# One step later for the softmax chain and the half ends, two for the terms, and single distances over a longer preparation

## What is computed

```
q    = grouped_conv1x1(bn(x), qw)                           # 8 groups of 16 channels
off  = tanh(pw @ gelu(depthwise_conv6x6_stride4(q))) * 4    # 8x8 sampling points a group
kv   = bilinear_sample(bn(x), grid + off);  k, v = conv1x1(kv)
pos  = grid_q - grid_kv                                     # 1024 queries x 64 keys x 2
bias = w3 @ relu(w2 @ relu(w1 @ (sign(pos) * log1p(|pos|)) + b1) + b2) + b3
out  = softmax(q k / 4 + bias) @ v;   x = x + out_w @ out;   x = x + mlp(bn(x))
```

## Time and profile before

| | before |
|---|---|
| median of 3 runs | 892.25 us (891.63 to 893.71) |
| the profiled execution: its own time, its span | 894.96 us, 893.2 us |
| PE busy | 820.4 us (92%) |
| DVE busy | 727.8 us (81%) |
| ACT busy | 662.1 us (74%) |
| GpSimd busy | 62.5 us (7%) |
| granted TensorE clock, mean | 0.983 |

### The profile page before, as it was taken

How to read it: one execution, slowest core, us unless ns; L and a number is a source line. 1 busy time by engine, 2 the same in 40 slices (tenths; PEclk the granted TensorE clock), 3 DMA queues, 4 the chain that set the end, 5 groups by cost and what they waited for, 6 DMA issues and landing times.

```text
span 893.2 us, 27554 instructions
## 1 busy us (share of the span) xinstructions
PE 820.4 (92%) x12486; PEld 235.6 (26%) x12486; DVE 727.8 (81%) x532; ACT 662.1 (74%) x742; POOL 62.5 (7%) x39
## 2 busy tenths in 40 slices
PE   4699998889999999988999999988999999999997
PEld 2222222222222222222222222222222222222224
DVE  5899898898868689799885879979888668989843
ACT  2468778968777688896776877797777668888863
POOL 1000101000010100101010010100101001010110
PEclk8699999999999999999999999999999999999999
DMA  4502020020200102002020200102002020200000
GB/s 167 118 3 49 2 48 3 12 66 2 63 15 17 34 3 49 12 19 49 2 62 15 48 1 14 37 12 57 11 5 60 14 48 3 73 3 3 3 15 24
DMA packets 18264, 27.67 MB, mean 31 GB/s; under 512 B 10980, under 2 KB 11620, under 8 KB 18148
## 3 DMA queue, kind: packets, MB, share of 16 engines
q1 hardware_dynamic: 18148, 25.91, 11.7%
HBM read 23.05 MB, written 2.74 MB: 29 GB/s over the span
## 4 chain that ended last, share of the span: by engine, by line
PE 68%; ACT 14%; DVE 10%; issue 7%; DMA 1%; SPq 0%; ACTq 0%; POOLq 0%
PE pair L887 24%; PE scores L905 22%; ACT h L481 7%; PE pair L861 6%; DVE h L629 5%; PE pair L1040 3%; PE scores L916 3%; PE pair L995 2%; DVE big L742 2%; PE pair L1031 2%; PE pair L1013 2%; PE scores L1001 1%; ACT big L548 1%; ACT big L577 1%; ACT L577 1%
## 5 line engine op out<-in xcount | busy, mean ns | idle before, releaser
L629 DVE TENSOR_TENSOR h<-hxy 128x2048 f32<-128x2048 f32 x256 | 582.6, 2303 | 71.8 <-PE pair L887 67.8
L481 ACT ACTIVATE h<-pair 128x1024 f32<-128x1024 f32 x512 | 518.7, 1025 | 154.3 <-PE pair L861 113.5
L887 PE MATMUL pair<-h,wts 32*32 32x512 f32 x8192 | 300.0, 604 | 20.7 <-DVE h L629 7.7
L905 PE MATMUL scores<-h,wts 128*32 128x512 f32 x2048 | 275.6, 608 | 0.1
L463 POOL CAST neg_max_wide<-neg_max 128x512 fp32r<-128x512 f32 x32 | 59.3, 1853 | 808.0 <-DVE neg_max L765 808.0
L861 PE MATMUL pair<-fy,u_rows 32*128 32x512 bf16 x1024 | 102.6, 387 | 0.0
L887 PEld LDWEIGHTS pair<-h,wts 32*32 32x32 f32 x8192 | 66.0, 103 | 82.1 <-ACT h L481 36.2
L861 PEld LDWEIGHTS pair<-fy,u_rows 32*128 32x128 bf16 x1024 | 26.4, 91 | 217.2 <-issue 217.2
L905 PEld LDWEIGHTS scores<-h,wts 128*32 128x32 f32 x2048 | 42.0, 108 | 156.2 <-issue 147.5
L995 PE MATMUL pair<-const,probs 128*128 128x128 f32 x128 | 20.1, 280 | 21.6 <-ACT h L481 20.8
L491 ACT ACTIVATE probs<-scores,wts 128x512 f32<-128x512 f32 x32 | 22.0, 689 | 23.7 <-PE scores L905 23.5
(11 more groups left out here) (106 smaller groups left out, 359.9 us busy)
## 6 DMA issues: line engine op xcount, KB each, us to landing
hxy<-features_dram SPq DMA_DIRECT2D x64, 256.0 KB, 4.8
wts<-weights_dram SPq DMA_DIRECT2D x2, 960.0 KB, 8.3
att_den<-reciprocals_dram SPq DMA_DIRECT2D x7, 256.0 KB
x<-x_dram SPq DMA_DIRECT2D x2, 512.0 KB, 5.7
fy<-fy_dram SPq DMA_DIRECT2D x16, 64.0 KB
fy_dram<-fy_part SPq DMA_DIRECT2D x24, 32.0 KB, 3.9
out_dram<-x SPq DMA_DIRECT2D x3, 256.0 KB, 5.4
features_dram<-pos_sign SPq DMA_DIRECT2D x4, 128.0 KB, 2.5
```

The costliest lines, as they stand in the source:

```text
L481: emptied("z", 2 * g + j, act.activation(h2[j][g % H2_BUFS][:].rearrange("p r n -> p (r n)"), pair_of("z", 2 * g + j)[:], ACT.Relu))
L629: dve.tensor_tensor(h1[g % H1_BUFS][:].rearrange("p c (y x) -> p c y x", x=W), hx[unit % 2][:, :, t].unsqueeze(2).broadcast_to([128, CT, H ...
L887: ins = pe.matmul(z_of(g, r)[32 * c:32 * (c + 1)], w(l, "w2")[key_rows(r), key_rows(r)], h1[g % H1_BUFS][key_rows(r), c], start=r >= 2, st ...
L905: ins = pe.matmul(scores[phase % 2][32 * r:32 * (r + 1)], w(l, "w3")[:, 32 * t:32 * (t + 1)], h2[rows[0] // 2][step % H2_BUFS][:, r % 2], ...
```

## The change

The softmax stages behind the copy, and all stages of `AFTER_SLOTS`, stand one step later; `fy_weights` and `hidden_terms` stand one and two steps later. `distances` now emits one activation a call and is called eight times instead of four, and the preparation from `image_t` on is given other steps, the last one 60 instead of 51. No instruction is added or left out. Cut, of the tables a line or two:

```diff
 BEFORE_SLOTS = {
...
-    ("act", "features", 0): 37, ("act", "spread_out", 0): 37, ("dve", "features_sign", 0): 40,
...
+    ("dve", "positions", 0): 39, ("pe", "spread", 0): 39, ("act", "features", 0): 38, ("act", "spread_out", 0): 39,
...
-SOFTMAX_SLOTS = {("pe", "scores_t"): 2, ("dve", "score_max"): 4, ("pool", "widen_max"): 3,
-                 ("pe", "max_off"): 4, ("act", "exp"): 4}
-TERMS_SLOT = 12
+SOFTMAX_SLOTS = {("pe", "scores_t"): 3, ("dve", "score_max"): 5, ("pool", "widen_max"): 4,
+                 ("pe", "max_off"): 5, ("act", "exp"): 5}
+TERMS_SLOT = 14
...
-    put("dve", 21, "fy_weights", 1)
+    put("dve", 22, "fy_weights", 1)
...
             def distances(n):
 
-                wait_emptied(act, "spread", n // 4)
-                for k in (2 * (n % 4), 2 * (n % 4) + 1):
-                    act.activation(hat_y[:, k], key_y, ACT.Abs, bias=cst("neg_y")[:, k:k + 1]).then_inc(distances_ready, 1)
+                k = n % CHUNKS
+                wait_emptied(act, "spread", n // CHUNKS)
+                act.activation(hat_y[:, k], key_y, ACT.Abs, bias=cst("neg_y")[:, k:k + 1]).then_inc(distances_ready, 1)
```

More of the change, by code:

```diff
@@ L83 @@
[L83 to L86, removed]
+    ("dve", "norm1", 0): 28, ("pe", "q", 0): 28, ("act", "q_out", 0): 28, ("dve", "conv_products", 0): 32,
+    ("dve", "conv_products", 1): 33, ("pe", "image_t", 0): 31, ("act", "image_t_out", 0): 31, ("dve", "conv_sum", 0): 34,
@@ new lines @@
+    ("dve", "conv_sum", 1): 35, ("act", "conv_gelu", 0): 35, ("pe", "offset", 0): 36, ("act", "offset_tanh", 0): 36,
+    ("dve", "positions", 0): 39, ("pe", "spread", 0): 39, ("act", "features", 0): 38, ("act", "spread_out", 0): 39,
+    ("dve", "features_sign", 0): 41, ("act", "distances", 0): 40, ("act", "distances", 1): 42,
+    ("act", "distances", 2): 43, ("act", "distances", 3): 44, ("act", "distances", 4): 46, ("act", "distances", 5): 47,
+    ("act", "distances", 6): 48, ("act", "distances", 7): 50, ("dve", "hats", 0): 47, ("dve", "hats", 1): 52,
@@ L87 @@
+    ("dve", "hat_products", 0): 48, ("dve", "hat_products", 1): 54, ("pe", "sample", 0): 55, ("dve", "sample_out", 0): 57,
+    ("pe", "keys_values", 0): 60, ("act", "keys_values_out", 0): 60,
 }
 AFTER_SLOTS = {
-    ("pe", "attend", 0): 5, ("act", "attend_out", 0): 5, ("dve", "reciprocal", 0): 9, ("dve", "divide", 0): 12,
-    ("pe", "project", 0): 12, ("dve", "residual1", 0): 14, ("pe", "mlp_up", 0): 14, ("act", "mlp_gelu", 0): 14,
-    ("pe", "mlp_up", 1): 15, ("act", "mlp_gelu", 1): 15, ("pe", "mlp_down", 0): 17, ("dve", "residual2", 0): 19,
-}
@@ L96 @@
-SOFTMAX_SLOTS = {("pe", "scores_t"): 2, ("dve", "score_max"): 4, ("pool", "widen_max"): 3,
-                 ("pe", "max_off"): 4, ("act", "exp"): 4}
-TERMS_SLOT = 12
+    ("pe", "attend", 0): 6, ("act", "attend_out", 0): 6, ("dve", "reciprocal", 0): 10, ("dve", "divide", 0): 13,
+    ("pe", "project", 0): 13, ("dve", "residual1", 0): 15, ("pe", "mlp_up", 0): 15, ("act", "mlp_gelu", 0): 15,
+    ("pe", "mlp_up", 1): 16, ("act", "mlp_gelu", 1): 16, ("pe", "mlp_down", 0): 18, ("dve", "residual2", 0): 20,
+}
@@ L100 @@
+SOFTMAX_SLOTS = {("pe", "scores_t"): 3, ("dve", "score_max"): 5, ("pool", "widen_max"): 4,
+                 ("pe", "max_off"): 5, ("act", "exp"): 5}
+TERMS_SLOT = 14
 PROLOGUE = {
     "pe": ["q", "image_t", "offset", "spread", "u_rows"],
-    "act": ["q_out", "image_t_out", "conv_gelu", "offset_tanh", "features", "spread_out"] + ["distances"] * 4,
+    "act": ["q_out", "image_t_out", "conv_gelu", "offset_tanh", "features", "spread_out"] + ["distances"] * 8,
     "dve": ["norm1", "w1y_rows", "conv_products", "conv_products", "conv_sum", "conv_sum", "positions", "features_sign",
```

## The result

The changed kernel takes 907.12 us (median of 4 runs, 906.37 to 908.18) against 892.14 (891.63 to 893.71) for the kernel before: a ratio of 1.0155 with a 95% interval of 1.0136 to 1.0174. It is **15 us slower**, where 13 us faster was forecast, and the result lies outside the forecast's range (868 to 889). The profiled execution took 908.18 us, its span is 906.4 us, and the mean granted clock fell from 0.983 to 0.968.

What follows compares the result with a forecast made beforehand. PE, busy 92% of the span, was taken to bound the kernel, so only its waits could move. Gains 5.7 + 6.0 + 1.1 + 0.9 - 0.7 = 13.0 off 892.25 gave 879.2 us, range 868 to 889.

Steps and rivals of the forecast that it cites:

- the last sentence on the quiet phases: Quiet phases: maxima, widening, `max_off` and exponential keep their distances from the transposes; no cost priced.
- The sentence on the terms: Terms two steps later: worth nothing; with cover gone they would cost up to 1.9 us a unit.
- quiet transposes: Quiet phases, softmax one step later: 19 transposes each gain 0.3 us of wait, 5.7 us, bounds 3.8 and 6.8.
- half ends: Half ends one step later: 0.35 us per half shrinks by 0.18, six halves, gain 1.1, bounds 0 and 2.1.
- The long waits at the transposes: Preparation, steps 35 and 43: waits of 2.05 and 1.65 us go; transposes' waits total 1.0 in place of 4.5.
- `spread`: Preparation, step 39: `spread` waits 2.3 us instead of 1.1 for a relu behind `features`; ends 0.1 and 3.5.
- Step 52: Preparation: PE's second layer waits 2.2 us for the maxima, against 1.8 for DVE before; ends 0 and 3.5.
- The clock: Each preparation: one fall to half clock, costing 1.7 us; ends 0 and 3.4.
- rival 1: Preparation gives its gain back: clock falls behind both long waits, `spread` waits its upper end; about 888 us, chance 0.18.
- the price of 884.3: Preparations: time in us if every wait as long as 2.05 us drew a clock fall, 3 x 1.7 more.
- Tail: End of the kernel: last maxima behind `divide` come 0.7 us later, a loss of 0.7, ends 0 and 1.5.
- Rival 3: Preparation, step 52: second `hats` wait for a late distance, holding first layer and maxima; 894 us or more, chance 0.08.

Runs made afterwards that it cites:

- version with the wait: The changed kernel plus a DVE wait, ahead of the second four products, for GpSimd's widening of that phase; 888.61 us, ratio 0.9944.
- version with both repairs: The changed kernel with DVE's second products waiting for GpSimd's widening, and `features` in step 39 instead of 38; 879.4 us, ratio 0.984.
- the filler runs: The fastest version plus one or three useless DVE instructions ahead of the maxima in seven phases of segment 3; 874.75 and 875.88 us.
- the fastest version: The changed kernel with `features` in 39, second `hats` in 53, all products (54, 56) behind a wait for the widening, `sample` 57; 874.15 us.

## Why the prediction was wrong

**The step that failed** is the last sentence on the quiet phases: "The maxima, the widening, `max_off` and the exponential keep their distances from the transposes." They do, in the tables, and so were priced at nothing. But the widening's *duration* is not its own: it depends on what DVE does behind the maxima. The cover that was not named was this: in every other phase of the old order the terms stood right behind the maxima, and in the rest the second first layer gave way to the cast or DVE paused ahead of it, so that no cast was longer than 2.62 us. The change moved the terms away and filled the time ahead of the maxima of 53, so that DVE reached them late, with four products and three first layers in a row behind them and none that gave way: casts of 9.42 us, 13.1 us of waits of PE in step 53 and a long fall of the clock in each preparation, 18.5 us in all by the run in which the products wait. The sentence on the terms ("nothing") is the same mistake.

Result and forecast lie 28 us apart (907.1 and 879.2). The 9.4 us that the collision in step 53 leaves open can be estimated from what follows: two falls of the clock more than priced in the version with the wait (3.4), step 37 (2.6), the quiet transposes (1.3) and the half ends (1.1), 8.4 together.

- *Quiet transposes* (forecast 5.7): right in mechanism. In the changed kernel they start 1.28 us after the second layer, without a wait:

```profile
816.65 1.17 PE L886 MATMUL pair<-h,wts 32*32 32x512 f32 x32
...
819.13 1.17 PE L886 MATMUL pair<-h,wts 32*32 32x512 f32 x32
820.41 0.63 PE L994 MATMUL pair<-const,probs 128*128 128x128 f32 x4
```

 instead of 1.55. But the step of the copy now lasts 2.48 instead of 2.42, which was not in the sum: steps 2 and 3 together fall from 5.86 to 5.63, 0.23 a phase, 4.4 for 19.
- *The long waits at the transposes*: gone, as said; 0.7 left in segment 1.
- *`spread`*: its wait was forecast at 2.3 and is 2.17, by the mechanism that was given (ACT of the changed kernel, the four instructions of `features` ahead of the relus):

```profile
372.78 0.41 ACT L527 ACTIVATE pos_abs<-pos 128x256 f32<-128x256 f32 x1
...
375.27 1.92 ACT L480 ACTIVATE h<-pair 128x1024 f32<-128x1024 f32 x2
...
376.42 2.02 PE L963 MATMUL pair<-const,coord 128*128 128x128 f32 x16 [2.17 <-ACT h L480]
```

- *Step 52*: its wait was forecast at 2.2 and is 1.97. *Step 36*: forecast 0.6, measured 0.42.
- *The clock*: one fall a preparation was priced (1.7). There were three, two and three, some of them 6.8 us long. The wait for the cast accounts for the long ones; but the product-wait version, without it, still has five falls in three preparations, behind `spread` and behind the maxima. So rival 1 was nearer here: without the collision in step 53 the change gives 888.61, near its 888, though only one half of its mechanism is there, as `spread` waits 2.17 us and not its upper end of 3.5. Nor does every wait as long draw a fall, as the price of 884.3 needs: `spread` waited 2.17 us in all three segments, and no fall followed in segment 1 (in the version with the wait, in segment 0).
- *Half ends* (forecast 1.1): not seen. Steps 0 to 27 of segments 1 to 3 shrink by 0.63 each, less than the four quiet transposes in them would give (0.92). The waits for the gelu are gone (2.0 us over six half ends), but `mlp_down` (L1039) now waits for a relu at each of the six, 1.8 us in all, and did not before. *`fy_weights`*: segment 0 shrinks by 1.89 there, 0.97 more than that 0.92, which fits the 0.9.
- *Tail* (forecast a loss of 0.7): 0.5. `divide` still sits behind its DMA, and the last maxima have lost their room of 1.75 us:

```profile
882.22 0.69 DVE L778 TENSOR_TENSOR work<-att_sum,att_den 128x512 f32<-128x512 f32 x1 [5.13 <-DMA att_den<-reciprocals_dram]
882.83 0.68 DVE L764 TENSOR_REDUCE neg_max<-pair 128x8 f32<-128x512 f32 x1
```

- *Rival 3*, the slower one, had the right price (PE waits over 3 us a preparation, and the clock falls a second time) one step too early, in 52, and the wrong mechanism: nothing waited for the hats.

The version with both repairs lands at 879.4, the forecast's figure, by chance: it removes a cost that the sum had counted (`spread`) along with the one that it had not.

## To carry to other kernels

Before moving a short GpSimd instruction that PE needs, look at what DVE does right behind its start: its length can be set by DVE's next break, and the break may be a stage that you are moving away. Where DVE is late, a break may not come in time; make a stage of DVE that is not urgent wait for GpSimd's result, which here cost 0.58 us of DVE's time a preparation and won 18.5 us in all. An engine that is not busy is no proof that its instruction is safe: GpSimd was idle for 93% of the span.

## What the hardware showed

**GpSimd gets no fair turn beside DVE.** The cast alone takes 0.62 us. Beside DVE it took 1.13, 1.54, 2.61, 4.81, 5.14, 7.01, 9.42 and up to 9.97 us: where DVE had more to do, it ended some 0.47 us after the end of a DVE instruction, but not always of the first one. In the nine traces in which GpSimd makes the widening, those with fillers left out, there are 141 phases in which two first layers follow the maxima. In 87 the second first layer gave way (2.70 us instead of 2.28) and the cast took 2.61; in 51 the cast was kept out past the second (4.81 or more); in three DVE paused behind the first. In all 51 DVE had come to the maxima without a break, in all 87 it had been idle for 0.17 us or more ahead of them. That looked like the cause, and the filler runs show that it isn't needed: without idle time right ahead the second first layer gave way as before. In those 51, DVE had run on for 4.85 us or more ahead of the maxima, with the fillers for 3.2 to 3.9, so a longer row is not excluded. What decides whether a DVE instruction that follows another at once gives way **stays open**. What is shown is that it can fail to, six times in a row in the changed kernel, and that a wait on DVE or another engine for the cast removes the loss where it stands. The casts of step 37 are 4.81 us long in the fastest version too, and cost PE 2.6 us there.

The Trainium skill ("SBUF — State Buffer", section "Who interferes with whom") says that a DVE instruction with two SBUF inputs and a GpSimd instruction that reads SBUF exclude each other for the whole instruction, and that the first to issue blocks the other. The traces agree with the exclusion (2.61 beside one first layer). They differ on the order: the record of the cast begins at 415.84, ahead of the products at 417.89 and of two more first layers, and the cast still ended behind all of them, at 425.26.
